# Recurrence of a six-sublayer decoder: the input product W_in as three fp16 products, with the low halves formed by VectorE

## The reference, cut to what matters

```python
gi = jnp.einsum('btd,hd->bth', x, W_in)          # W_in is 1024 x 256
gate, xc = jnp.split(gi, 2, axis=-1)
...                                              # causal convolution of xc over 4 taps, per channel
g = jnp.einsum('bth,gh->btg', xc, W_g) + b_g     # W_g is 1024 x 512
forget, inp = jnp.split(g, 2, axis=-1)
alpha = jnp.exp(ALPHA_LOG_SCALE * jax.nn.softplus(forget_base) * jax.nn.sigmoid(forget))
beta = jnp.sqrt(1.0 - alpha ** 2 + 1e-06)
bterm = beta * jax.nn.sigmoid(inp) * xc
_, h = lax.associative_scan(_scan_combine, (alpha, bterm), axis=1)
out = jnp.einsum('bth,dh->btd', jax.nn.gelu(gate, approximate=False) * h, W_out)
```

## Time and profile before

| | |
|---|---|
| median of 3 runs | 1240.49 us (1237.5 to 1240.51) |
| the profiled execution: own time | 1238.5 us |
| its span, first to last instruction | 1236.7 us |
| mean granted TensorE clock | 0.935 of 2.4 GHz |
| TensorE busy | 1064.0 us (86% of the span) |
| VectorE busy | 959.4 us (78%) |
| ScalarE busy | 692.3 us (56%) |
| GpSimd busy | 382.4 us (31%) |

### The profile page before, as it was taken

The page is one execution under the profiler, slowest core; times in us unless marked ns, Lnnn a source line. Parts: engine busy times, 40 slices in busy tenths (PEclk is TensorE's granted clock), DMA queues, the critical chain, the costliest instruction groups (busy, mean ns, idle before and its releaser), DMA issues. The chain is left out here.

```text
span 1236.7 us, 30089 instructions
## 1 busy us (share of the span) xinstructions
PE 1064.0 (86%) x10763; PEld 854.4 (69%) x10763; DVE 959.4 (78%) x2126; ACT 692.3 (56%) x1461; POOL 382.4 (31%) x535
## 2 busy tenths in 40 slices
PE   4899989999998799986279999489999849998796
PEld 3578778778787577765257777377878737776685
DVE  7688878877887588987937884669998658989597
ACT  3454444444545255555637776367778625555684
POOL 5122222221230256552220000414322225655232
PEclk9899999999999899997569999699999969999899
DMA  7000000200000230003336531300000000000011
GB/s 263 10 10 2 10 13 2 84 3 2 3 2 2 82 126 12 22 9 157 137 127 247 178 110 43 113 23 19 25 17 21 1 14 15 20 22 9 18 54 50
DMA packets 33493, 64.29 MB, mean 52 GB/s; under 512 B 7524, under 2 KB 23268, under 8 KB 30308
## 3 DMA queue, kind: packets, MB, share of 16 engines
q1 hardware_dynamic: 31844, 58.57, 13.5%
q0 software_dynamic: 1536, 4.20, 1.1%
HBM read 43.03 MB, written 12.39 MB: 45 GB/s over the span
## 5 line engine op out<-in xcount | busy, mean ns | idle before, releaser
L1151 ACT ACTIVATE ca_pth<-ca_turned 77x512 f16<-77x512 f32 x128 | 75.8, 592 | 101.3 <-PE ca_turned L1293 101.3
L395 ACT ACTIVATE wa_probs<-wa_scores,wa_minus_top 128x192 f32<-128x192 f32 x256 | 83.1, 436 | 80.0 <-DVE wa_minus_top L488 80.0
L1094 POOL TENSOR_TENSOR ca_z<-ca_z,ca_top 128x308 f32<-128x308 f32 x128 | 87.9, 698 | 113.5 <-DVE ca_top L1189 113.5
L351 POOL TENSOR_TENSOR wa_q<-wa_by_cos,wa_by_sin 128x256 f32<-128x256 f32 x32 | 23.3, 729 | 264.7 <-DVE wa_by_sin L483 264.7
L1194 DVE SCALAR_TENSOR_TENSOR ca_ptl<-ca_turned,ca_pth 77x512 f16<-77x512 f32 x128 | 87.0, 680 | 20.4 <-ACT ca_pth L1151 20.4
L1293 PE MATMUL ca_turned<-ident,ca_probs 128*77 128x128 f32 x512 | 87.0, 294 | 14.0 <-ACT ca_probs L1143 13.9
L406 ACT ACTIVATE wa_pth<-wa_turned 128x384 f16<-128x384 f32 x128 | 58.3, 505 | 72.5 <-PE wa_turned L715 72.5
L1293 PEld LDWEIGHTS ca_turned<-ident,ca_probs 128*77 128x77 f32 x512 | 57.4, 151 | 44.6 <-ACT ca_probs L1143 24.6
L640 PE MATMUL wa_scores<-wa_xh,wa_wh 128*128 128x256 f16 x256 | 70.9, 277 | 10.6 <-DVE wa_wl L467 8.7
L488 DVE TENSOR_REDUCE wa_minus_top<-wa_scores 128x2 f32<-128x384 f32 x128 | 62.3, 548 | 20.3 <-PE wa_scores L703 18.1
L715 PE MATMUL wa_turned<-ident,wa_probs 128*128 128x128 f32 x512 | 68.3, 275 | 7.8 <-ACT wa_probs L395 3.9
(11 more groups left out here) (388 smaller groups left out, 3639.1 us busy)
## 6 DMA issues: line engine op xcount, KB each, us to landing
ex_stage<-in_ew SPq DMA_DIRECT2D x16, 1024.0 KB, 7.0
slots<-slots_zeros SPq DMA_DIRECT2D x10, 512.0 KB, 6.1
ca_xs<-tokens SPq DMA_DIRECT2D x16, 256.0 KB, 2.4
ex_xe<-slots SPq DMA_DIRECT2D x11, 320.0 KB, 3.3
slots<-ex_y SPq DMA_DIRECT2D x9, 320.0 KB
wa_x_stage<-in_xt SPq DMA_DIRECT2D x8, 256.0 KB, 3.1
tokens<-in_x SPq DMA_DIRECT2D x1, 2048.0 KB, 15.3
ca_w<-in_xw SPq DMA_DIRECT2D x2, 1024.0 KB, 6.3
```

The costliest lines, as they stand in the source:

```text
L395: ins = act.activation(probs[2 * (u % 2) + t][:, h, t * WINDOW:t * WINDOW + SPAN], s_bank[i][:, t * SPAN:(t + 1) * SPAN], ACT.Exp, bias=mi ...
L1094: pool.tensor_tensor(z[k][:, heads], z[k][:, heads], top[:, k, heads].unsqueeze(2).broadcast_to((P, UH, CTX)), ALU.subtract).then_inc(shif ...
L1151: act.activation(pth[k][0:CTX], t_bank[k][0:CTX], ACT.Copy, scale=PSCALE).then_inc(probs_high, 1)
```

## The change

The product with W_in becomes three fp16 products, as the gates have them already: high tokens by high weights, low tokens by high weights, high tokens by low weights, summed in PSUM. The tokens `re_xt` become `re_xth` (ScalarE, fp16 of 1024 x) and `re_xtl` (VectorE, the rest), the weights `re_w_in` become `re_w_ih` and `re_w_il`. `way_in` waits for VectorE now. The load of `w_in` moves from the routing stage into the experts, and its split stands behind the last unit, ahead of the split of `w_g`. The readers of `re_in` scale the result back.

```diff
@@ experts
             unit(0, 0, 0, loads=True)
+            gates.load_in(sp)
             gates.load_gates(sp, w_g)
...
             all_units(act, unit)
+            gates.split_in_high(act)
             gates.split_high(act, w_g)
...
             take_y(end - 1)
+            gates.split_in_low(dve)
             gates.split_low(dve, w_g)
@@ class Gates
-        sp.dma_start(self.w_in[:], w_in_dram).then_inc(self.w_loaded, 16)
...
+    def split_in_high(self, act):
+        act.wait_ge(self.in_loaded, 16)
+        for g in range(KT_):
+            act.activation(self.w_ih[:, g], self.w_in[:, g], ACT.Copy, scale=SCALE).then_inc(self.in_high, 1)
+
+    def split_in_low(self, dve):
+        for g in range(KT_):
+            dve.wait_ge(self.in_high, g + 1)
+            dve.scalar_tensor_tensor(out=self.w_il[:, g], in0=self.w_in[:, g], scalar=SCALE, in1=self.w_ih[:, g],
+                                     op0=ALU.mult, op1=ALU.subtract).then_inc(self.in_low, 1)
@@ recurrence, ScalarE
-                act.activation(xt[:], x_bank[:], ACT.Copy).then_inc(x_ready, 1)
+                act.activation(xth[:], x_bank[:], ACT.Copy, scale=SCALE).then_inc(x_high, 1)
...
-                tile(b, 2)
-                if enters:
-                    tokens(b + 2)
+                tile(b, 2, between=(lambda: tokens(b + 2)) if enters else None)
                 tile(b, 3)
@@ recurrence, VectorE
+            def tokens_low(b):
+                dve.wait_ge(x_high, b + 1)
+                dve.scalar_tensor_tensor(out=xtl[:], in0=x_bank[:], scalar=SCALE, in1=xth[:],
+                                         op0=ALU.mult, op1=ALU.subtract).then_inc(x_ready, 1)
...
+                if enters:
+                    tokens_low(b + 2)
                 scale_input(b, par, 1)
                 decay(b, 1)
...
             dve.wait_ge(cleared, 1)
+            tokens_low(0)
             convolve(0, 0, 0)
+            tokens_low(1)
             convolve(0, 0, 1)
@@ recurrence, TensorE
                         for g in range(KT_):
-                            ins = pe.matmul(i_bank[s % 2][:, k], w_in[:, g, m * P:(m + 1) * P], xt[:, g],
-                                            start=(g == 0), stop=(g == KT_ - 1))
+                            for w, x in ((w_ih, xth), (w_ih, xtl), (w_il, xth)):
+                                ins = pe.matmul(i_bank[s % 2][:, k], w[:, g, m * P:(m + 1) * P], x[:, g],
+                                                start=(n == 0), stop=(n == 3 * KT_ - 1))
+                                n += 1
```

More of the change, by code:

```diff
@@ L1869, in experts @@
         w_g = sb("w_g", [P, HT, 2 * HID])
+        gates.hold(ctx, nc)
         passed = sb("passed", [P, 1])
@@ L2095, in sem @@
             return ctx.enter_context(nc.semaphore("re_" + name))
-        self.w_in = sb("w_in", [P, KT_, 2 * HID])
         self.w_out = sb("w_out", [P, HT, DIM])
@@ L2105, in __init__ @@
         self.g_loaded = sem("g_loaded")
+        self.w_ih = ctx.enter_context(nc.sbuf_tensor("re_w_ih", [P, KT_, 2 * HID], F16))
+        self.w_il = ctx.enter_context(nc.sbuf_tensor("re_w_il", [P, KT_, 2 * HID], F16))
+        self.in_loaded = sem("in_loaded")
+        self.in_high = sem("in_high")
+        self.in_low = sem("in_low")
         self.w_gh = ctx.enter_context(nc.sbuf_tensor("re_w_gh", [P, HT, 2 * HID], F16))
@@ L2118, in load, with load_in, hold @@
         sp.dma_start(self.hid[:], hid_dram).then_inc(self.hid_loaded, 16)
-        sp.dma_start(self.w_in[:], w_in_dram).then_inc(self.w_loaded, 16)
+        self.w_in_dram = w_in_dram
         self.w_g_dram = w_g_dram
         sp.dma_start(self.w_out[:], w_out_dram).then_inc(self.w_loaded, 16)
+    def load_in(self, sp):
+        sp.dma_start(self.w_in[:], self.w_in_dram).then_inc(self.in_loaded, 16)
+    def hold(self, ctx, nc):
+        self.w_in = ctx.enter_context(nc.sbuf_tensor("re_w_in", [P, KT_, 2 * HID], F32))
     def load_gates(self, sp, w_g):
@@ L2185, in sem @@
             return ctx.enter_context(nc.semaphore("re_" + name))
-        w_in, w_gh, w_gl, w_out, hid, half_bias, rate = (gates.w_in, gates.w_gh, gates.w_gl, gates.w_out, gates.hid,
+        w_ih, w_il, w_gh, w_gl, w_out, hid, half_bias, rate = (gates.w_ih, gates.w_il, gates.w_gh, gates.w_gl, gates.w_out, gates.hid,
                                                          gates.half_bias, gates.rate)
@@ L2193, in recurrence @@
         xs = [sb(f"xs{k}", [P, TPB, DIM]) for k in range(2)]
-        xt = sb("xt", [P, KT_, SEQ])
+        xth = sb("xth", [P, KT_, SEQ], F16)
+        xtl = sb("xtl", [P, KT_, SEQ], F16)
         padded = sb("padded", [P, HT, TAPS - 1 + SEQ])
@@ L2226, in recurrence @@
         x_turned = sem("x_turned")
+        x_high = sem("x_high")
         x_ready = sem("x_ready")
@@ L2358, in gated_input, with tile @@
                     act.wait_ge(in_done, 4 * b + 2 + p + 1)
-                    act.activation(gate[par][:, 2 * p:2 * p + 2], i_bank[p][:], ACT.Gelu).then_inc(in_read, 1)
-            def tile(b, m):
+                    act.activation(gate[par][:, 2 * p:2 * p + 2], i_bank[p][:], ACT.Gelu, scale=UNSCALE).then_inc(in_read, 1)
+            def tile(b, m, between=None):
                 p, k = divmod(m, 2)
@@ L2369, in tile @@
                 act.activation(ti[p][:, k], g_bank[m][:, 1], ACT.Tanh, scale=GSCALE, bias=half_bias[:, 1, m:m + 1]).then_inc(ti_done, 1)
+                if between:
+                    between()
                 act.wait_ge(tf_done, b * HT + m + 1)
@@ L2541, in _ @@
         def _(pe):
-            pe.wait_ge(gates.w_loaded, 32)
+            pe.wait_ge(gates.w_loaded, 16)
+            pe.wait_ge(gates.in_low, KT_)
             def turn(b, par):
```

4 lines of the change are left out of this document (3 added, 1 removed).

## The result

| | before | changed |
|---|---|---|
| median of 20 runs each | 1238.86 us (1236.13 to 1240.8) | 1241.11 us (1239.72 to 1244.86) |
| ratio, 95% interval | | 1.0019 [1.0012, 1.0026] |
| span of the profiled execution | 1236.7 us | 1239.4 us |

The page of the changed kernel, busy time by engine, shows what was meant: TensorE has 13 us less to do than before, VectorE 6 us more.

The account below looks back on a forecast made before the run. Round bound by VectorE from `re_d` to `re_gh`, TensorE's way out and tile 2, ScalarE's tiles 2 and 3. Splits 2.3, steady rounds 0.3, start 0.3, clock 1.7: 1240.49 + 4.6 = 1245.1 us, range 1239.5 to 1251.5.

Parts of the forecast that it names:

- Splits +2.3: End of the experts: two more VectorE splits lock out GpSimd's `ex_passed`, so gathers and barrier come 2.3 us later.
- Rival A: End of the experts: GpSimd gets in at a split boundary; 1242.8 us, 1241.1 if batch 0's clock holds; chance 0.22.
- Clock +1.7: Way out of batch 0: about 2.8 us of TensorE idle time lowers its clock, costing 1.7 us; steady rounds nothing.
- Start of the recurrence +0.3: First batches: gate tile 0 1.6 us late, 1.2 given back by the vanished `re_padded` wait; +0.3 us, bounds -0.9 and +1.6.
- Steady rounds +0.3: Six steady rounds: `tokens_low` fills VectorE's 0.61 us idle time; 0.05 us a round for rounding, +0.3 us.
- the way in is not in it: Steady rounds: the way in is outside the loop, it only has to give `re_padded` in time for the convolution.
- C: Recurrence rounds: the way in bounds them, seven rounds give 1.1 us each, less 2.3 for splits; 1235 us; chance 0.07.
- D: Steady rounds: VectorE becomes late by its new instruction, +0.3 to 0.6 us a round; 1247 to 1249 us; chance 0.10.
- the load of `w_in`: Experts' loads: about 5.5 us of transfer join; costed at nothing, up to 5.5 us if an expert waited for weights.
- B: Steady rounds: TensorE's new idle time ahead of the way out costs 1.7 us of clock; 1248.5 to 1255; chance 0.16.

Follow-up runs that it names:

- e7: Changed kernel with the split of `w_in` moved inside the last expert units, between their activations; ratio 1.0019 to the kernel before.
- e1: Changed kernel with the marker behind the last store (`ex_passed`) computed by ScalarE instead of GpSimd; ratio 1.0014 to the kernel before.
- e3: Changed kernel with ten matmuls whose result is never used ahead of each way out; ratio 0.9993 to the kernel before.
- e9: e7 with one wait more: GpSimd starts `re_bterm` only behind the first half of VectorE's convolution; ratio 0.9969 to the kernel before.
- e5: Changed kernel without the third product (low weights by high tokens), 32 matmuls a way in instead of 48; ratio 1.0067 to the kernel before.
- e8: Changed kernel with `tokens_low` ahead of the two low halves of the convolution in each batch; ratio 1.0091 to the kernel before.
- e10: Changed kernel without the third product, with 24 unread matmuls ahead of each way out and GpSimd's wait for the convolution; ratio 0.9971 to the kernel before.
- e11: Changed kernel, `w_in` split in last expert units, last two `w_g` splits behind the gathers, unread matmuls ahead of ways out, GpSimd's wait for the convolution; ratio 0.9973.
- e13: Changed kernel with only GpSimd's wait for the first half of the convolution; ratio 0.9997 to the kernel before.
- e15: e9 with 10 unread matmuls ahead of each way out as well; ratio 0.9997 to the kernel before.
- e14: Kernel before with only GpSimd's wait for the first half of the convolution; ratio 1.0002 to the kernel before.
- e16: Kernel before, fp32 way in, with the early token copy and GpSimd's wait for the convolution; ratio 0.9966 to the kernel before.
- e4: Kernel before with the early token copy alone (ahead of gate tile 2's third activation), fp32 way in; ratio 0.9991 to the kernel before.

## Why the prediction was off in size

1. *Splits +2.3.* Right: +2.25, and e7 took it back. Rival A is refuted, and e1 shows that the lock also holds up GpSimd's issuing of a transfer. That the measured median, 1241.11 us, is rival A's figure with the clock kept, 1241.1, is chance: neither of its two conditions came true.
2. *Clock +1.7, at the way out of batch 0 alone.* Right: C2 is +1.69, e3 returns it. The exact hit has some luck in it, since the clock held behind 2.74 us of idle time in e9.
3. *Start of the recurrence +0.3.* This term was mis-sized: -0.59 (B + C1). `re_d` of batch 0 was 1.16 us late, where I had the tiles 1.6 us late; VectorE waited 1.67 us for `re_xth` of batch 1, not 2 to 3. What is given back is 1.75, not 1.2: on top of the wait of 1.19 us came the second `rn_res`, 0.97 us before and 0.51 now. I had counted waits only and not looked at how long VectorE's instructions take beside GpSimd's.
4. *Steady rounds +0.3.* Mis-sized too: -0.71 (D + E). The late `re_padded` is there (in two rounds VectorE comes 0.2 us later to the first `rn_res`), but the way in ends earlier, the second copy of `re_padded` with it, and the second `rn_res` shrinks from 0.81 to 0.56. Together this gives 0.42 us over four rounds, and the scan's shorter wait for `re_bterm` gives the other 0.34 in the fifth. The step that failed is "the way in is not in it", the loop. It is, through ScalarE's order (`re_padded` ahead of `re_beta`), GpSimd's `re_bterm` and the lock, at 0.15 us a round (D / 5).
5. *Rivals.* C did not happen as stated: the way in matters, but by 0.15 us a round and not by 1.1. D did not happen; the load of `w_in` (7.8 us to landing, `w_g` 14.0 instead of 10.9) delayed no expert unit. B did not happen here, but stood next door: 0.8 us and more of added idle time ahead of a way out, in e5 and e8, came with a way out that took 1.4 us longer or more.

So +4.6 became +2.65 in the profile by two terms, 0.9 and 1.0 us too high, of one cause: I had counted VectorE's waits and not how long its instructions take beside GpSimd's. The measured 2.3 us agree, as far as single profiles can tell. What stays open: stretch F took 242.1 to 245.4 us in kernels that run the same code there. One part is the clock behind the 3.55 us of idle time at its end, which held in e9, e10 and e11 and fell in all the others; why, and what gave the rest, was not tried. A difference of 2 us between two kernels can lie in F, and one of 1.7 us in E; this bears on e9, e13 and e15, and on how much of e9's 0.9969 is the guard's. That GpSimd gets in first in a part of the changed kernel's executions would explain e13 as well; no profile shows it.

## What to carry to other kernels

Where two engines share a lock, put their long instructions one behind the other with a wait, rather than let the schedule decide: one wait gave 1.8 us in batch 0's round (e9 against e7), and where it wasn't needed it cost at most 0.2 us from A to E (e14, e13, e16 against e4). Before taking work from an engine that isn't the bound, look at the idle time that this leaves ahead of its work on the critical loop: in e5 it grew to 2.8 us and more, TensorE's clock fell in each round, and the shorter way in became a loss of 8 us. Compare the durations of the same instruction in different rounds as well as the waits: a loop can lose time where no row shows an idle engine. And before a gain of 2 us in one profile is put down to an edit, look at the granted clock in the stretches that the edit does not touch.
